# Order of TensorE's work in the first attention: transposes of a batch, scores of the next, outputs

## The reference

```python
q = jnp.einsum('bsd,od->bso', query, W) + b
attn_logits = jnp.einsum('bqd,bkd->bqk', q, memories) + add_mask   # 100 x 1444 a batch
attn_weights = jax.nn.softmax(attn_logits, axis=-1)
attn_outputs = jnp.einsum('bqk,bkd->bqd', attn_weights, memories)
x = x + attn_outputs
```

## Time and profile before

| what | us |
|---|---|
| median of 3 runs | 2559.65 |
| lowest and highest run | 2558.86, 2561.89 |
| the profiled execution, its own time | 2562.09 |
| its span in the trace | 2559.9 |
| scores of the first batch begin | 28.8 |
| last addition of the first attention ends | 182.3 |
| mean granted TensorE clock over the span | 0.913 |

### The profile page before, as it was taken

How to read it: one execution, slowest core, us unless ns; L and a number is a source line. 1 busy time by engine, 2 the same in 40 slices (tenths; PEclk the granted TensorE clock), 3 DMA queues, 4 the chain that set the end, 5 groups by cost and what they waited for, 6 DMA issues and landing times. The chain is left out here.

```text
span 2559.9 us, 45852 instructions
## 1 busy us (share of the span) xinstructions
PE 2152.0 (84%) x18128; PEld 1500.8 (59%) x18128; DVE 1289.9 (50%) x1666; ACT 1453.6 (57%) x1758; POOL 236.4 (9%) x305
## 2 busy tenths in 40 slices
PE   4767978969879569999747999979966999986998
PEld 2544845847548246666435666646754666654787
DVE  4552343334333466666466777744136666643211
ACT  2334445445454558888636888853235888872332
POOL 1005023141330400000010000010010000000000
PEclk9997989989989789999868999978987999995999
DMA  5758336354462558888137778720034777720000
GB/s 175 229 174 300 142 135 222 117 193 176 164 217 107 166 120 186 187 187 187 33 88 162 182 183 188 174 61 1 0 78 108 182 182 184 188 70 1 21 21 21
DMA packets 119703, 352.73 MB, mean 138 GB/s; under 512 B 20122, under 2 KB 54800, under 8 KB 118896
## 3 DMA queue, kind: packets, MB, share of 16 engines
q1 hardware_dynamic: 105728, 322.40, 46.5%
q0 software_dynamic: 13776, 27.54, 3.7%
HBM read 257.58 MB, written 91.23 MB: 136 GB/s over the span
## 5 line engine op out<-in xcount | busy, mean ns | idle before, releaser
L944 ACT ACTIVATE a_probs<-a_score 128x1200 f32<-128x1200 f32 x768 | 857.8, 1169 | 202.7 <-PE a_score L857 202.6
L857 PE MATMUL a_score<-a_qstack,a_kstack 128*128 128x400 f32 x2304 | 551.8, 371 | 57.0 <-DVE a_qstack L1027 55.9
L857 PEld LDWEIGHTS a_score<-a_qstack,a_kstack 128*128 128x128 f32 x2304 | 379.5, 190 | 227.1 <-issue 180.0
L819 PE MATMUL a_numer<-a_probs,a_v 128*18 128x200 f32 (+1 forms) x9216 | 470.2, 334 | 0.0
L819 PEld LDWEIGHTS a_numer<-a_probs,a_v 128*18 128x18 f32 (+1 forms) x9216 | 228.2, 97 | 183.5 <-issue 87.6
L1018 DVE TENSOR_TENSOR a_kstack<-a_kraw,a_kstack 64x2888 fp32r<-64x2888 f32 x90 | 284.8, 3165 | 2.8
L1027 DVE TENSOR_TENSOR a_qstack<-a_qrep,k_groupmask 128x1600 fp32r<-128x1600 f32 x48 | 87.6, 1826 | 172.1 <-PE a_score L857 143.1
L1013 DVE CAST a_kstack<-a_kraw 128x2888 fp32r<-128x2888 f32 x90 | 149.9, 1665 | 10.7 <-DVE a_own L1078 9.3
L1484 ACT ACTIVATE f3d_hidden<-f3d_ph,f_b 128x400 f32<-128x400 f32 x128 | 75.9, 593 | 117.5 <-PE f3d_ph L1442 110.2
L1694 PEld LDWEIGHTS f0r_ph<-f0r_xsT,f0r_w 128*128 128x128 f32 x896 | 119.5, 199 | 30.6 <-issue 12.6
L1694 PE MATMUL f0r_ph<-f0r_xsT,f0r_w 128*128 128x128 f32 x896 | 123.4, 283 | 9.3 <-DVE f0r_xsT L1870 9.3
(11 more groups left out here) (360 smaller groups left out, 2788.2 us busy)
## 6 DMA issues: line engine op xcount, KB each, us to landing
a_kraw<-keys SPq DMA_DIRECT2D x384, 361.0 KB, 6.3
values<-kv_vst SPq DMA_DIRECT2D x32, 1296.0 KB
a_v<-values SPq DMA_DIRECT2D x48, 864.0 KB, 6.0
keys<-kv_made SPq DMA_DIRECT2D x48, 722.0 KB
l0a_ctxT<-in_ctxT SPq DMA_DIRECT2D x16, 722.0 KB, 6.7
kv_ctxT<-in_ctxT SPq DMA_DIRECT2D x16, 722.0 KB, 6.7
l0a_ctx<-in_ctx SPq DMA_DIRECT2D x16, 704.0 KB
l0a_mask<-in_mask_BxSxS_ik SPq DMA_DIRECT2D x16, 564.1 KB
```

The costliest lines, as they stand in the source:

```text
L819: last = pe.matmul(numer[32 * g:32 * g + PC, p * 2 * SQ:(p + 1) * 2 * SQ], v[0:rows(t), j, t, (2 * g + p) * PC:(2 * g + p + 1) * PC], prob ...
L857: last = pe.matmul(to, kstack[:, j, g * SK + t * 128:g * SK + (t + 1) * 128], qstack[:, j, g * GH:(g + 1) * GH, :], start=True, stop=not s ...
L944: act.activation(probs[:, n % NP, :].rearrange("p (g q) -> p g q", g=SPAN), slot_ps[:, n % 2, :, 0:GQ], ACT.Exp, scale=HSCALE).then_inc(ex ...
```

## The change

`outputs` on PE is cut in two. Its first half, the wait for the exponentials and the 12 transposes, becomes `turns(b, j)`. Its second half keeps the name. PE then makes, for every batch, T of b first, then S of b+1, then O of b. Instructions and waits are the same ones, in another order; no other engine's list changes.

```diff
-            def outputs(b, h, j):
+            def turns(b, j):
                 pe.wait_ge(exped, b + 1)
                 for t in range(KT):
                     last = pe.transpose(ps[0:rows(t), j, t * 128:t * 128 + SQ],
                                         probs[:, j, t * 128:t * 128 + rows(t)], k.ident[0:SQ, 0:SQ])
                 last.then_inc(turned, 1)
+
+            def outputs(b, h, j):
                 pe.wait_ge(kept, b + 3)
                 pe.wait_ge(ctx_in[j], 32 * h + 32)
                 pe.wait_ge(added, b + 1)
...
             scores(0, 0, 0)
             with pe.Fori(0, (B - 2) // 2) as i:
+                turns(2 * i, 0)
                 scores(2 * i + 1, i, 1)
                 outputs(2 * i, i, 0)
+                turns(2 * i + 1, 1)
                 scores(2 * i + 2, i + 1, 0)
                 outputs(2 * i + 1, i, 1)
+            turns(B - 2, 0)
             scores(B - 1, B // 2 - 1, 1)
             outputs(B - 2, B // 2 - 1, 0)
+            turns(B - 1, 1)
             outputs(B - 1, B // 2 - 1, 1)
```

## The result

| what | before | after |
|---|---|---|
| median of 4 runs, us | 2560.77 | 2585.49 |
| lowest and highest, us | 2558.86, 2562.50 | 2585.18, 2588.55 |
| span of the profiled execution, us | 2559.9 | 2583.5 |
| first S to last addition's end in the first attention, us | 153.5 | 177.7 |
| clock from 51 to 170 us | 1.00 | 0.82 |

The ratio is 1.0094, with a 95% interval of 1.0082 to 1.0106. The changed stage alone, from the first S to the end of the last addition, is 24.2 us longer (row four of the table), so the rest of the program gives nothing that has to be explained. The forecast was 2580.6.

What follows compares the result with a forecast made beforehand. No engine was full; a chain of hand-overs set 9.00 us a period. Circle +1.0, start +0.0, last batch -0.1 and clock +20 gave +21 us, so a median of 2580.6 us, range 2558 to 2588.

Steps and rivals of the forecast that it cites:

- The old circle: First attention before the change: S, T, copies, O, addition, `q1`, 9.00 us a period; logits, maximum and exponentials lie beside it.
- The copies, the addition and `q1` leave the path: First attention: copies (1.21 us) run beside S, O ends at 5.7 us, addition and `q1` are done at about 7.0.
- The new circle: First attention after the change: S, logits, maximum, exponentials, T, S takes 9.08 us (8.83 to 9.60), +1.0 us over 13 periods.
- T and the waits: Terms on PE between T and the next S: 1.05 us for 12 transposes, 0.15 for three satisfied waits (0 to 0.42).
- The hand-over from ACT to PE: Semaphore step from the end of ACT's accumulator read to T on PE, taken as 0.16 us (0.06 to 0.26).
- The ends: First and last batches of the attention: start about equal, 11.3 against 11.28 us, no gain; last batch -0.1 us.
- The tail: Last batch: T starts 7.88 us after S against 7.97, -0.1 us; T, copies, O and addition then as before.
- Transfers: SP's loads in the first attention: same order, context loads about 2.3 us earlier in the period, masks in time, cost nothing.
- The clock: PE's break of about 2.2 us before T lowers the clock in 12 of 15 batches, 1.7 us each: 20 us.
- Rival A: First attention: the clock falls in most breaks before T; 2580.6 us, from 2568 to 2589; chance 0.62.
- rival B: First attention: the clock stays up despite one 2.2 us break a period; 2560.5 us, from 2557 to 2567; chance 0.31.
- eight of eight: Elsewhere in the earlier trace, all eight PE breaks of 1.85 to 2.37 us begun at full clock were followed by half clock.

Runs made afterwards that it cites:

- The run with three products: Changed kernel plus three idle products of 384 columns on PE behind O of every batch: 2560.18 against 2562.25 us for the kernel before, ratio 0.9991.

## Why the prediction was right

*The old circle* was read rightly. Logits in three parts moved nothing in the old order.

*The copies, the addition and `q1` leave the path.* They did. In the period after, DVE finishes `q1` at 58.98, 1.7 us before the S that needs it, and O starts as S ends.

*The new circle* was put at 9.08 us, with 8.83 as the lower end, and is 8.81 at the full clock. The terms of the chain held: 2.70 to the logits, 3.38 to the exponentials, 1.60 to the end of the accumulator read. T and the waits were too dear: T to S takes 1.08 in all where 1.05 + 0.15 stood, so the three satisfied waits cost next to nothing. The hand-over from ACT to PE is 0.05 (84.97 to 85.02) instead of 0.16. With 13 periods that is -2.5 us instead of +1.0.

*The ends.* From the second S to the third: 11.14 us after (38.99 to 50.13), 11.28 before, as forecast about equal. The tail was put at -0.1 and is not. T and O of the last batch ran at the low clock, which had set in just before T, and from T to the last addition it took 8.15 us (197.38 to 205.53), where it was 5.67 before, from the T at 176.30 to the addition of this line:

```profile
181.97 0.35 DVE L414 SCALAR_TENSOR_TENSOR k_x<-l0a_py,l0a_inv,k_x 100x128 f32<-100x128 f32 x1 [5.14 <-PE l0a_py L337]
```

In the old order nothing fell there. This is a part of the falls' price that I had counted only for T and S.

*Transfers* cost nothing, as forecast. At a period of 10.7 us they were less pressed than before, DMA share 0.63 against 0.73. That is a weaker test than the forecast's period of 9.1 us. The run with three products gives it: DVE waited on the mask 7 times there, 7.1 us in all, and S to S stayed at 8.81. At 7.67 the masks did hold the circle.

*The clock* was the term that decided. The forecast took 12 falls of 1.7 us; there were 15. Over the 13 periods the loss is 13 x (10.68 - 8.81) = 24.3 us, 1.87 each. That is 1.7 in most, and about twice as much once, where T and S both ran at 0.50 (T at 122.41, S at 124.46 with 4.81). The tail adds 0.5 before T and 2.5 behind it. The whole stage: -0.4 ahead of the second S, whose context landed a little earlier, -0.1, 24.3 - 2.5, 0.5 and 2.5 make +24.3, against 24.2 in the traces. By the warning of the Trainium skill ("TensorE: Matmul & The Clock Gate", section "Why this matters for your kernels") the clock would have stayed up. It was too mild here: the trace disagrees with it 15 times, at 2.35 us each.

*What was luck.* The forecast of +20.9 us came near +24.2 because its errors went opposite ways. The clock cost 24.3 + 0.5 + 2.5 = 27.3 us and not 20. The circle was 3.5 us cheaper than the +1.0 it was put at.

Rival A held, rival B did not. That the break does it and not the order is shown from both sides: filling it in the new order brings the time back, and stretching it in the old order brings falls there. What was wrong is the reading of the length. I had taken 1.85 us as the shortest break with a fall behind it and 1.34 as harmless. The clock fell after 9 and 11 of 15 breaks of 1.53 and 1.59 us, while after 2.45 to 2.71 us it fell in 4 of 16, and one fall came behind 0.77 and 1.34 us. So "eight of eight" was no rule of the length, and that all 15 fell at 2.35 us is more than it could promise. (Of those eight, the break at 1695.77 is not the last in time; one of 1.90 us at 2293.84 is, with the same outcome.)

What else decides is open. The runs differ in their period and in what stands beside the break, and none of them separates the two. The rows also leave a third candidate: when a break comes, and not only how long it is. In the kernel after, the breaks are all alike, but the drop comes some 0.25 us earlier against T from one batch to the next (T is 1.27, 1.52 and 1.76 us at 59.55, 70.06 and 80.56), and with one idle product the falls came by threes. So something with a beat of its own may have a part. No run varied this by itself.

## What to carry to other kernels

Moving work so that an engine's idle pieces join into one can cost more than the schedule gains: add up PE's breaks after the move, and look in the same trace for breaks of that length and what the clock did behind them. When the clock is in play, judge a schedule by its S to S distance at the full clock, and fill the break with idle products before giving the order up. Here the better order was 0.19 us a batch faster as a schedule, and only together with a shorter chain on DVE was the whole kernel measurably faster.

## What the runs showed of the hardware

- A break on PE of 1.53 us, the only one in its period of 8.81 us, was followed by the lower clock level in 9 of 15 cases; 1.59 us in 11 of 15; 2.35 us in 15 of 15; 1.21 us in none of 9. In another order, with a second break of 0.73 to 1.03 us in each period, 1.87 and 2.13 us did it in 8 of 16, 2.45 and 2.71 us in only 4 of 16, and 1.34 to 1.65 us in none of 16. All these are counts of single executions.
- A fall cost some 1.7 us of the path when it hit T and S, which are on it: 10.5 us from one T to the next instead of 8.81. Two cases cost more: 3.2 us where T and S both ran low, and 2.5 us behind the last T.
- PE passed three satisfied semaphore waits between T and S with no visible gap: 1.08 us from the first of 12 transposes to S, where the transposes' loads alone take 1.02.
- A float32 product of 384 columns takes 0.7 us at the full clock (4 in 2.82), as two records of 0.35.
